# Four transformer blocks on one core: the last heads' queries and keys as one paired matmul, and the last stage's opening beside the last gated batch

## The chip, the cores and the metric

The kernel runs on one core of a Trainium2 chip, in one launch. The metric is the device time in microseconds from the first to the last instruction. TensorE multiplies matrices into PSUM (eight banks of 128 partitions by 512 fp32 values), ScalarE and VectorE read PSUM and SBUF, GpSimd works on SBUF alone, and the Sync engine issues the DMAs. Each engine works through its own instructions in order and waits on semaphores for the others.

## The reference, cut to what matters

The input is x, 4 batches of 512 tokens by 320, with a context of 512 by 192 for each batch. The stages, numbered as in the kernel:

```python
# 0, 1: attention on tokens, then on context: 20 heads of 64; 2: gated feed-forward
# 3, 4: the same with 20 heads of 16;                         5: gated feed-forward
x = attend(layer_norm(x), layer_norm(x), 20 heads of 16) + x      # stage 3
x = attend(layer_norm(x), ctx, 20 heads of 16) + x                # stage 4
# 6: two attentions on 16 + 16 tokens of the context, each weighed by a gate
out = anat_gate * attend(q, k_anat, v_anat) + dis_gate * attend(q, k_dis, v_dis)
x = out @ w_out.T + b_out + x
# 7: attention on the context without a layer norm: 20 heads of 16
q, k, v = heads(x @ Wq), heads(ctx @ Wk), heads(ctx @ Wv)
x = softmax(q k / sqrt(16)) v @ Wo + bo + x
```

## The kernel before, in words

All values are fp32 but for some copies in bf16. x stays in SBUF for the whole kernel. Each engine has its instructions written out by hand: one function for each engine and kind of stage, all looping over the same numbered steps.

A **narrow round** n (stages 3 and 4 are rounds 0 to 7 of run "r3", stage 7 is rounds 0 to 3 of run "r7") treats one batch in 20 steps i. The 20 heads form five groups u of four, one head in each strip of 32 partitions; i = 4u + kb, with kb one of four blocks of 128 keys. In a step TensorE does, in this order (`narrow_steps_pe`): two *row scores* (bf16, queries by 512 keys, for the maxima of a group to be treated six steps later), the *column scores* of this step (`cols_pe`, fp32, 128 keys by 512 queries for four heads, into banks 0 to 3), two more row scores, and then inserts of other work: queries Q, keys K, values V of a chunk, the product of probabilities and values (`mix`), transposes of the output (`turn`, `out`), the output matmul (`y`). ScalarE takes the exponentials of the column scores (`exp_act4`, two halves of 1024 columns) and copies out of PSUM, VectorE the maxima of the row scores (`rows_dve4`), GpSimd casts queries and keys to bf16. The queries of a chunk hold eight heads, and are written twice by ScalarE, each time with a mask that zeroes the other head of each pair of 16 partitions. The last four heads (group 4, columns 256 to 320 of the weights) are laid out twice in the weights, so that chunk 2 is 128 wide as well and one masked activation does (mask column 2). Keys get an additive mask (columns 3 to 5). Queries and keys of chunks 0 and 1 are made in the round before (steps 10 to 18), chunk 2 in steps 0 and 2 of the round itself.

An insert that needs a bank takes the next of four in turn (`Turns.choose`); `wait_free` waits until the bank's former use is over, `wait_full` and `wait_out` for a named item to be written, or taken out again. For the narrow runs the four are banks 4 to 7, and row scores take part in the turn.

The steps of round -1 are the *opening* of a run: transposes of x (steps 3, 4, 6) and of the context (7, 8), Q0 (10), K0 (12), V0 (14), V1 (15), Q1 (16), K1 and the transposed maxima `negm` (18), V2 (19), and from step 14 on the row scores of round 0, four in each step. Run r3 has its opening beside the output phase of stage 2 (`out_pe`, table MEET). Run r7 has it by itself, after the gated stage.

The **gated stage** (6) has steps g = 4n + i for four batches n and token blocks i. In step g TensorE transposes the probabilities of g - 2 (`g_turn_pe`, L1854), makes the scores of g (`g_scores_pe`, L1847, into banks 0 and 1), does a piece of the next batch's set-up, and makes the output of g - 2 (`g_y_pe`, L1901). VectorE takes the probabilities of g - 1 (`g_probs_dve`), the maximum of g and the subtraction (`g_max_dve`), and adds the output of g - 2 (`g_y_dve`, two instructions). The last batch is g = 12 to 15, and 16 and 17 have no scores. The semaphore `sub` counts the subtractions, so its sixteenth means that banks 0 and 1 are read.

The names in the profile: L1059 column scores, L1072 row scores, L1084 maxima, L1251 Q, L1276 K, L1302 V, L1107 the transposed maxima, L1126 mix, L1097 exponentials, L1204 and L1231 transposes of x and of the context, L595 probabilities by values of the wide stages 0 and 1, L351 the feed-forward's output. One fp32 matmul of the program is two passes in the trace, one bf16 matmul or transpose is one.

## Time and profile before

| | us |
|---|---|
| median of 3 runs | 3333.94 (3331.95 to 3334.76) |
| the profiled execution | 3336.34, span 3334.6, mean granted clock 0.989 |
| TensorE busy | 3214.7 (96%) |
| TensorE weight loads, beside the matmuls | 1462.8 (44%) |
| VectorE, ScalarE, GpSimd busy | 1737.4, 1476.5, 805.1 |
| DMA | 62.32 MB, mean 19 GB/s |

Busy time is the union of an engine's instructions. The span is the profiled core's; the time of an execution lies a little above its span. The change touches stages 3, 4, 6 and 7, all after 1763 us.

### The profile page before, as it was taken

What the parts mean: (1) busy time and instruction counts of PE and PEld (TensorE: products, weight loads), DVE (VectorE), ACT (ScalarE), POOL (GpSimd) and SP (SyncE); (2) the same over time, 40 slices, a digit from 0 to 9 for tenths busy, and PEclk for the clock granted to TensorE, in tenths of its full rate; (3) what the DMA queues carried; (4) which work ended last, traced back from release to release, by engine and by line L of the source; (5) the groups of instructions that cost most, each with busy time, mean ns of one, the idle gap of its engine ahead of it and who ended that gap; (6) DMA issues with size and microseconds to landing.
All of it is one profiled execution on the core that took longest, in us unless ns stands there. A gap on an engine that the chain in (4) does not pass through costs nothing.

```text
span 3334.6 us, 39289 instructions
## 1 busy us (share of the span) xinstructions
PE 3214.7 (96%) x15478; PEld 1462.8 (44%) x15478; DVE 1737.4 (52%) x2568; ACT 1476.5 (44%) x1983; POOL 805.1 (24%) x620
## 2 busy tenths in 40 slices
PE   7999999999999999999999999999999999989997
PEld 3344344443434343435444344444434545643443
DVE  2645455454555555552234677777762222656664
ACT  3544444445454545441112656666652112326664
POOL 2544444454554554550000000000000000000000
PEclk9999999999999999999999999999999999989999
DMA  3000000000100000000000000000002000000000
GB/s 110 24 16 20 16 17 20 23 19 20 58 18 18 17 23 13 16 24 20 0 5 26 1 1 1 30 11 6 1 23 65 1 0 33 1 5 6 14 9 17
DMA packets 37284, 62.32 MB, mean 19 GB/s; under 512 B 7024, under 2 KB 24944, under 8 KB 36208
## 3 DMA queue, kind: packets, MB, share of 16 engines
q1 hardware_dynamic: 37104, 59.82, 5.9%
q8 instruction: 125, 2.05, 0.3%
q14 instruction: 55, 0.45, 0.0%
HBM read 57.19 MB, written 2.62 MB: 18 GB/s over the span
## 4 chain that ended last, share of the span: by engine, by line
PE 89%; DVE 5%; ACT 4%; issue 1%; POOL 0%; DMA 0%; ACTq 0%; DVEq 0%; POOLq 0%
PE bank L1589 9%; PE bank L510 9%; PE bank L595 9%; PE bank L1126 7%; PE bank L737 5%; PE bank L351 5%; PE bank L673 5%; PE bank L1059 4%; PE bank L1251 3%; PE bank L676 3%; PE bank L709 3%; PE bank L1276 3%; PE bank L1179 2%; PE bank L533 2%; DVE heads L1084 2%; PE bank L1594 2%
## 5 line engine op out<-in xcount | busy, mean ns | idle before, releaser
L1084 DVE TENSOR_REDUCE heads<-bank 128x1 f32<-128x512 f32 x960 | 598.3, 683 | 237.2 <-PE bank L1072 236.4
L544 DVE TENSOR_REDUCE heads<-bank 128x2 f32<-128x1024 f32 x320 | 392.4, 1226 | 594.7 <-PE bank L533 594.7
L581 POOL TENSOR_TENSOR heads<-heads,probs 128x1024 f32<-128x1024 f32 x160 | 389.5, 2434 | 12.5
L567 ACT ACTIVATE probs<-bank 128x1024 f32<-128x1024 f32 x320 | 328.0, 1025 | 130.3 <-PE bank L519 130.0
L577 POOL TENSOR_TENSOR heads<-probs 128x1024 f32<-128x1024 f32 x80 | 190.7, 2384 | 712.8 <-ACT probs L567 712.8
L510 PE MATMUL bank<-heads 64*128 64x512 f32 x1280 | 335.7, 602 | 0.1
L1059 PE MATMUL bank<-heads 32*128 32x512 f32 x1920 | 296.8, 628 | 25.8 <-ACT weights L1097 10.9
L595 PE MATMUL bank<-probs,values 128*64 128x512 f32 x1280 | 294.0, 601 | 1.4 <-ACT nmT L558 1.0
L1589 PE MATMUL bank<-hT,weights 128*128 128x512 f32 x640 | 291.8, 606 | 1.5 <-issue 1.5
L1097 ACT ACTIVATE weights<-bank 128x1024 f32<-128x1024 f32 x236 | 228.8, 1022 | 96.0 <-PE bank L1059 93.9
L1652 ACT ACTIVATE ctx_in<-bank,b_col 128x512 f32<-128x512 f32 x80 | 55.1, 688 | 419.4 <-PE bank L1594 323.8
L1072 PE MATMUL bank<-heads 32*128 32x512 bf16 x960 | 214.6, 387 | 26.7 <-DVE heads L1084 7.4
L1269 POOL CAST heads<-heads 128x512 bf16<-128x512 f32 x60 | 35.6, 616 | 842.2 <-ACT heads L1260 842.2
L1671 DVE SCALAR_TENSOR_TENSOR mixed<-bank,b_col,ctx_in 128x512 f32<-128x512 f32 x80 | 60.1, 751 | 258.1 <-ACT ctx_in L1652 142.7
L1589 PEld LDWEIGHTS bank<-hT,weights 128*128 128x128 f32 x640 | 119.6, 192 | 165.3 <-issue 163.8
L1097 ACT ACTIVATE probs<-bank 128x1024 f32<-128x1024 f32 x164 | 159.0, 1022 | 62.6 <-PE bank L1059 61.9
L684 ACT COPY heads<-bank 128x512 f32<-128x512 f32 x160 | 93.7, 585 | 187.8 <-PE bank L673 167.7
L351 PE MATMUL bank<-weights,mixed 128*128 128x320 f32 x640 | 175.4, 432 | 0.0
L1072 PEld LDWEIGHTS bank<-heads 32*128 32x128 bf16 x960 | 63.7, 92 | 237.5 <-issue 112.1
L673 PE MATMUL bank<-hT,heads 128*128 128x512 f32 x320 | 161.7, 628 | 0.0
L595 PEld LDWEIGHTS bank<-probs,values 128*64 128x64 f32 x1280 | 85.2, 137 | 172.4 <-issue 168.1
L291 POOL TENSOR_SCALAR vare<-mv 128x4 f32<-128x4 f32 x24 | 4.7, 195 | 577.7 <-DVE mv L277 488.3
(205 smaller groups left out, 4868.9 us busy)
## 6 DMA issues: line engine op xcount, KB each, us to landing
heads<-in_wqk SPq DMA_DIRECT2D x40, 320.0 KB, 2.8
heads<-in_wqk SPq DMA_DIRECT2D x40, 256.0 KB, 2.6
weights<-in_L_xattn_w_ff SPq DMA_DIRECT2D x3, 1600.0 KB, 7.2
weights<-in_L_xattn_ff_w SPq DMA_DIRECT2D x3, 1600.0 KB, 7.1
ctx_in<-in_ctx SPq DMA_DIRECT2D x12, 384.0 KB, 3.7
weights<-in_L_xattn_qkv_q SPq DMA_DIRECT2D x2, 1632.0 KB, 7.4
weights<-in_L_xattn_wo SPq DMA_DIRECT2D x2, 1600.0 KB, 12.2
x_res<-in_x SPq DMA_DIRECT2D x4, 640.0 KB, 13.3
```

The lines of the kernel that those rows point to most:

```text
L351: last = nc.tensor.matmul(M.bank[QUARTER[t]][:, 0:D], v["OT"][c][:, t * P:t * P + P], v["wo"][:, c, :], start=c == 0, stop=c == NF - 1)
L510: nc.tensor.matmul(cols[:, g, :], v["KT"][strip, U % 2, kb * P:kb * P + P], v["QT"][strip, U % 2, :], start=True, stop=False)
L544: nc.vector.tensor_reduce(v["negm"][:, U % 2, qb, :].rearrange("p (g k) -> p g k", g=2)[:, :, 0], M.ROWS[:, :, :], AX.X, ALU.max, negate=T ...
L567: nc.scalar.activation(v["probs"][:, kb, :, :], M.COLS[kb % 2][:, :, :], ACT.Exp, scale=float(r.work[n][0].prm["dh"]) ** -0.5).then_inc(r. ...
L581: nc.gpsimd.tensor_tensor(ps, ps, pr[:, k, :, :], ALU.add).then_inc(r.sem("part"), 1)
L595: last = nc.tensor.matmul(bank[64 * g:64 * g + 64, :], v["V"][:, kb, 2 * u + g, :], v["probs"][:, kb, g, :], start=kb == 0, stop=kb == TB - 1)
L673: last = nc.tensor.matmul(q[:, :], w[:, e, :], M.hT[:, e, :], start=False, stop=e == 1)
L1059: last = nc.tensor.matmul(M.QUAD[:, g, :], v["KT"][strip, u, kb * P:kb * P + P], v["QT"][strip, u, :], start=True, stop=True)
L1072: nc.tensor.matmul(r.bank_of(item, m)[:, :], v["QB"][strip, u, qb * P:qb * P + P], v["KB"][strip, u, :], start=True, stop=True).then_inc(r ...
L1084: nc.vector.tensor_reduce(v["negm"][:, tile, qb, 32 * h + at:32 * h + at + 1], r.bank_of(item, m)[:, :], AX.X, ALU.max, negate=True).then_ ...
L1097: nc.scalar.activation(v["probs"][g % slots][:, 2 * h:2 * h + 2, :], M.QUAD[:, 2 * h:2 * h + 2, :], ACT.Exp, scale=float(r.work[n][0].prm[ ...
L1589: last = nc.tensor.matmul(bank[:, :], v["w1"][:, j, 2 * part + e, :], M.hT[:, e, :], start=first and e == 0, stop=(not first) and e == 1)
```

## The change

Two things are changed. First, `QK_pe4` takes the place of Q2 and K2 in each narrow round: 64 columns of query weights write partitions 0 to 63 of one bank, 64 columns of key weights partitions 64 to 127, by turns. One ScalarE copy takes both into the tile `tail`, and GpSimd writes the masked queries and keys of group 4 from it, 64 partitions at a time, and casts them. V3 moves from step 0 to step 2. Second, the 20 steps of r7's opening are spread over g = 12 to 17 of the gated stage by the tables MEET_FRONT (ahead of the output of g - 2) and MEET_BACK (behind it). While they run, row scores take banks 0 and 1 by turns and the other items banks 6 and 7; the gated outputs keep to banks 2 and 3. The gated stage's second set of W and O moves to other places in SBUF.

```diff
+        self.tail = self.heads[:, 10240:10752]
...
                 if i == 0 and now:
-                    items += [("Q2", n), ("V3", n)]
+                    items += [("QK2", n)]
...
                 if i == 2 and now:
-                    items += [("K2", n)]
+                    items += [("V3", n)]
...
+        class GuestRun(Run):
+            def choose(self, name, n, i):
+                if n >= 0:
+                    return Run.choose(self, name, n, i)
+                if name[0:3] == "row":
+                    return 4 + int(name[7]) % 2
+                return 2 + sum(bank < 4 for bank, _ in self.place.values()) % 2
...
+            if n == 0 and i == 0:
+                for h in (2, 3):
+                    r.wait_out(pe, f"row1_1_{h}", 0)
...
+        def QK_pe4(pe, r, n):
+            s, v, bank = r.work[n][0], n_view(r, n), r.bank_of("QK2", n)
+            r.wait_free(pe, "QK2", n)
+            for e in range(3):
+                for home, name, x, ch in ((bank[0:64, :], "wq", M.hT, CH3), (bank[64:P, :], "wk", kvT(s), keys(s))):
+                    if e < len(ch):
+                        last = nc.tensor.matmul(home, v[name][0:ch[e][1], e, 256:320], x[0:ch[e][1], e, :], start=e == 0, stop=e == len(ch) - 1)
+            last.then_inc(r.full("QK2", n), 1)
+        def QK_act4(act, r, n):
+            r.wait(act, "q_tail", 2 * n)
+            r.wait(act, "k_tail", 2 * n)
+            r.wait_full(act, "QK2", n)
+            nc.scalar.copy(M.tail[:, :], r.bank_of("QK2", n)[:, :]).then_inc(r.free("QK2", n), 1)
+        def Q_tail_pool(pool, r, n):
+            v, low, high = n_view(r, n), slice(0, 64), slice(64, P)
+            r.wait(pool, "cols", 20 * n)
+            r.wait(pool, "q_cast", 5 * n)
+            r.wait_out(pool, "QK2", n)
+            r.wait(pool, "k_cast", 5 * n + 4)
+            for out, which in ((low, 0), (high, 1)):
+                r.wait(pool, "q_tail", 2 * n + which)
+                nc.gpsimd.tensor_scalar(v["QT"][out, 4, :], M.tail[low, :], M.mask[low, which:which + 1], M.mask[low, 6:7], ALU.mult, ALU.add
+                                        ).then_inc(r.sem("q_tail"), 1)
+            r.wait(pool, "q_tail", 2 * n + 2)
+            nc.gpsimd.tensor_copy(v["QB"][:, 4, :], v["QT"][:, 4, :]).then_inc(r.sem("q_cast"), 1)
...
+        MEET_FRONT = {12: (0, 5), 13: (5, 7), 14: (8, 9), 15: (11, 13), 16: (15, 16), 17: (17, 18)}
+        MEET_BACK = {13: (7, 8), 14: (9, 11), 15: (13, 15), 16: (16, 17), 17: (18, 20)}
...
                         g_setup_pe(pe, r, n + 1, SETUP[i][0])
+                    if g == 12:
+                        for k in range(2):
+                            r.wait(pe, f"free{k}", r.count[k])
+                    if g in MEET_FRONT:
+                        narrow_steps_pe(pe, r.guest, -1, *MEET_FRONT[g])
                     if 0 <= g - 2 < 4 * r.N:
                         g_y_pe(pe, r, g - 2)
+                    if g == 15:
+                        r.wait(pe, "sub", 16)
+                    if g in MEET_BACK:
+                        narrow_steps_pe(pe, r.guest, -1, *MEET_BACK[g])
...
                     if 0 <= g - 2 < 4 * r.N:
                         g_y_dve(dve, r, g - 2)
+                    if g == 13:
+                        narrow_begin_dve(dve, r.guest)
+                    if g in MEET_BACK:
+                        narrow_steps_dve(dve, r.guest, -1, *MEET_BACK[g])
...
-                7: Run("r7", stages[7:8], M.NX, 20)}
+                7: GuestRun("r7", stages[7:8], M.bank[4:8] + M.bank[0:2], 20, led=True)}
```

`K_tail_pool` is `Q_tail_pool` for the keys, with the upper half of `tail` and the key mask as the added scalar. The ScalarE loop gets the two tables in the same way as TensorE's, ahead of and behind its exponential.

TensorE, steps 0 to 2 of a round of stage 3 (row scores L1072, column scores L1059, then Q2 and V3 in step 0 and K2 in step 2), before:

```order
L1072 MATMUL bank<-heads 128x512 x2
L1251 MATMUL bank<-hT,weights 128x512 x3
L1302 MATMUL bank<-weights,hT 128x320 x3
L1072 MATMUL bank<-heads 128x512 x2
L1059 MATMUL bank<-heads 128x512 x4
L1072 MATMUL bank<-heads 128x512 x4
L1059 MATMUL bank<-heads 128x512 x4
L1072 MATMUL bank<-heads 128x512 x2
L1276 MATMUL bank<-hT,weights 128x512 x3
L1107 MATMUL bank<-ident,heads 128x128 x4
```

and of the change (row scores are now L1087, column scores L1074, the paired group L1319, values L1359):

```order
L1087 MATMUL bank<-heads 128x512 x2
L1319 MATMUL bank<-hT,weights 64x512 x6
L1087 MATMUL bank<-heads 128x512 x2
L1074 MATMUL bank<-heads 128x512 x4
L1087 MATMUL bank<-heads 128x512 x4
L1074 MATMUL bank<-heads 128x512 x4
L1087 MATMUL bank<-heads 128x512 x2
L1359 MATMUL bank<-weights,hT 128x320 x3
L1122 MATMUL bank<-ident,heads 128x128 x4
```

The values have moved from step 0 to the place of the keys in step 2, and six matmuls with 64 output partitions stand where three queries stood.

TensorE at the end of the gated stage in the change (turns L1912, outputs L1959; of the opening row scores L1087, values L1359, Q L1266, K L1291, transposed maxima L1122), from the output in step 15 to the one in step 17:

```order
L1959 MATMUL bank<-weights,mixed 128x320 x5
L1087 MATMUL bank<-heads 128x512 x4
L1359 MATMUL bank<-weights,cT 128x320 x2
L1912 MATMUL bank<-ident,mixed 128x128 x5
L1087 MATMUL bank<-heads 128x512 x4
L1359 MATMUL bank<-weights,cT 128x320 x2
L1959 MATMUL bank<-weights,mixed 128x320 x5
L1087 MATMUL bank<-heads 128x512 x4
L1266 MATMUL bank<-hT,weights 128x512 x3
L1912 MATMUL bank<-ident,mixed 128x128 x5
L1087 MATMUL bank<-heads 128x512 x4
L1959 MATMUL bank<-weights,mixed 128x320 x5
```

Before, three outputs and two turns follow each other here, and the row scores come only after all of them. VectorE in the same stretch of the change (probabilities L1941 to L1949, output additions L1966 and L1969, maxima L1099), from step 15's addition on:

```order
L1966 TENSOR_TENSOR ysum<-bank,heads 128x320
L1969 TENSOR_TENSOR x_res<-ysum,x_res 128x320
L1099 TENSOR_REDUCE heads<-bank 128x1 x4
L1941 TENSOR_REDUCE mixed<-mixed 128x40
L1943 RECIPROCAL probs<-mixed 128x40
L1946 TENSOR_TENSOR probs<-probs,heads 128x40
L1949 TENSOR_TENSOR mixed<-mixed,probs 128x640
L1099 TENSOR_REDUCE heads<-bank 128x1 x4
L1966 TENSOR_TENSOR ysum<-bank,heads 128x320
L1969 TENSOR_TENSOR x_res<-ysum,x_res 128x320
L1099 TENSOR_REDUCE heads<-bank 128x1 x8
```

The maxima stand behind the additions and behind the last probabilities.

## Rows read from the trace of the kernel before

**Rows 1.** The page: busy time by engine, and the chain by engine.

```profile
PE 3214.7 (96%) x15478; PEld 1462.8 (44%) x15478; DVE 1737.4 (52%) x2568; ACT 1476.5 (44%) x1983; POOL 805.1 (24%) x620
...
PE 89%; DVE 5%; ACT 4%; issue 1%; POOL 0%; DMA 0%; ACTq 0%; DVEq 0%; POOLq 0%
```

**Rows 2.** Timeline, round 1 of stage 3: start, duration, engine, line, passes [idle before].

```profile
1908.12 1.78 PE L1302 MATMUL bank<-weights,hT 108*128 108x320 f32 x6
...
1909.84 1.24 PE L1059 MATMUL bank<-heads 32*128 32x512 f32 x8
...
1915.96 2.85 PE L1276 MATMUL bank<-hT,weights 108*128 108x512 f32 x6
...
1918.64 0.60 PE L1107 MATMUL bank<-ident,heads 128*128 128x128 f32 x4
```

**Rows 3.** Timeline, a round of stage 4, steps 0 to 3.

```profile
2264.65 1.24 PE L1302 MATMUL bank<-weights,cT 96*128 96x320 f32 x4
...
2265.82 1.24 PE L1059 MATMUL bank<-heads 32*128 32x512 f32 x8
...
2272.03 1.94 ACT L1097 ACTIVATE probs<-bank 128x1024 f32<-128x1024 f32 x2 [0.30 <-PE bank L1059]
2272.10 1.98 PE L1276 MATMUL bank<-cT,weights 96*128 96x512 f32 x4
...
2274.46 1.24 PE L1059 MATMUL bank<-heads 32*128 32x512 f32 x8
```

**Rows 4.** Timeline, a wide round: probabilities by values, two heads side by side.

```profile
1215.69 3.65 PE L595 MATMUL bank<-probs,values 128*64 128x512 f32 x16
```

**Rows 5.** Groups of GpSimd, shapes apart: count | busy us, mean ns | idle before.

```profile
L581 POOL TENSOR_TENSOR heads<-heads,probs 128x1024 f32<-128x1024 f32 x160 | 389.5, 2434 | 12.5
...
L1269 POOL CAST heads<-heads 128x512 bf16<-128x512 f32 x60 | 35.6, 616 | 842.2 <-ACT heads L1260 842.2
...
L291 POOL TENSOR_SCALAR vare<-mv 128x4 f32<-128x4 f32 x24 | 4.7, 195 | 577.7 <-DVE mv L277 488.3 <-DVE mv L1511 52.4 <-DVE mv L922 36.9
```

**Rows 6.** Timeline, round 1 of stage 7: column scores of steps 0 and 10.

```profile
3065.93 1.19 PE L1059 MATMUL bank<-heads 32*128 32x512 f32 x8
...
3110.01 1.24 PE L1059 MATMUL bank<-heads 32*128 32x512 f32 x8
```

**Rows 7.** Timeline, gated steps 14 and 15: turn, output, next turn.

```profile
2925.60 0.71 PE L1854 MATMUL bank<-ident,mixed 128*128 128x128 f32 x5
...
2929.39 2.86 PE L1901 MATMUL bank<-values,mixed 128*128 128x320 f32 x10
2932.09 0.71 PE L1854 MATMUL bank<-ident,mixed 128*128 128x128 f32 x5
```

**Rows 8.** Timeline, the opening of stage 7.

```profile
2947.40 1.47 PE L1204 MATMUL bank<-ident,x_res 128*108 128x128 f32 x12
...
2957.50 0.40 PE L1072 MATMUL bank<-heads 32*128 32x512 bf16 x4 [2.26 <-issue]
...
2965.58 4.93 PE L1251 MATMUL bank<-hT,weights 108*128 108x512 f32 x6 [0.20 <-DVE heads L1084]
...
2982.45 2.31 PE L1059 MATMUL bank<-heads 32*128 32x512 f32 x8
```

**Rows 9.** Timeline, VectorE in the same opening.

```profile
2970.86 4.88 DVE L1084 TENSOR_REDUCE heads<-bank 128x1 f32<-128x512 f32 x8 [3.54 <-PE bank L1072]
```

**Rows 10.** Windows: length, busy (instructions) by engine, TensorE's granted clock, DMA.

```profile
2957.00:2961.00 4.00, 2.67 (x11) 1.01 (x11) 2.48 (x4) 0.43 (x1) 0.96 (x2) 0.82 0.00 2
2961.00:2965.00 4.00, 3.85 (x10) 1.48 (x9) 2.65 (x5) 0.43 (x1) 0.00 (x0) 0.50 0.00 0
```

**Rows 11.** Timeline: stage 3's opening, first and last, and an output phase alone.

```profile
1763.91 1.47 PE L1204 MATMUL bank<-ident,xn 128*108 128x128 f32 x12
...
1817.84 2.06 PE L1059 MATMUL bank<-heads 32*128 32x512 f32 x8
...
2780.65 21.70 PE L351 MATMUL bank<-weights,mixed 128*128 128x320 f32 x80
```

More of the change, by code:

```diff
@@ L250, in program @@
              ("VT", 3 * P, "p (c k) -> p c k", dict(c=3)), ("wg", 2, *one), ("sc", 4, *one), ("wgb", 2 * P, "p (c k) -> p c k", dict(c=2)),
[L251 to L254 removed]
+             ("heads8", 8, *one), ("sev", B, *one), ("shift", B, *one),
+             *[(name, 2 * B, "p (b k) -> p b k", dict(b=B)) for name in ("arg", "ge")], ("W", 3 * 640, "p (c k) -> p c k", dict(c=3)))
+        take(M.heads[:, 9216:10752], ("bo", D, *one), ("gate", 2 * B, "p (b k) -> p b k", dict(b=B)))
+        take(M.values[:, 0:1600], ("O", 5 * D, "p (c f) -> p c f", dict(c=5)))
+        take(M.values[:, 3200:5200], ("Kbd", 640, *one), ("Vbd", 640, *one))
         take(M.mixed, ("hT", 2 * 3 * N, "p (s c n) -> p s c n", dict(s=2, c=3)), ("S", 2 * 640, "p (s k) -> p s k", dict(s=2)), ("PT", 640, *one),
@@ L257, in program @@
         take(M.probs[:, 0, 0, :], ("fac", 40, *one), ("gfac", 40, *one))
-        G["W"] = [G["W"][:, k, :, :] for k in range(2)]
-        G["O"] = [G["O"][:, k, :, :] for k in range(2)]
+        G["W"] = [G["W"], M.weights[:, 8512:10432].rearrange("p (c k) -> p c k", c=3)]
+        G["O"] = [G["O"], M.weights[:, 6464:8064].rearrange("p (c f) -> p c f", c=5)]
         GS = M.pair[0].rearrange("p b k -> p (b k)")
@@ L388, in __init__ @@
                         for item in self.step_items(n, i):
-                            bank = self.choose(item[0], i)
+                            bank = self.choose(item[0], n, i)
                             self.place[item] = (bank, count[bank])
@@ L393, in __init__ @@
                         self.upto[steps * n + i] = tuple(count)
-            def choose(self, name, i):
-                return len(self.place) % len(self.banks)
+                self.count = count
+            def choose(self, name, n, i):
+                return len(self.place) % 4
             def sem(self, what):
@@ L1258, in Q_act4 @@
             r.wait_full(act, item, n)
-            for u, which in ((2 * c, 0), (2 * c + 1, 1)) if c < 2 else ((4, 2),):
+            for u, which in ((2 * c, 0), (2 * c + 1, 1)):
                 last = nc.scalar.activation(v["QT"][:, u, :], r.bank_of(item, n)[:, :], ACT.Identity, bias=M.mask[:, 6:7],
@@ L1265, in Q_pool4 @@
             v = n_view(r, n)
-            r.wait_full(pool, f"row{min(2 * c + 1, 4)}_3_3", n - 1)
+            r.wait_full(pool, f"row{2 * c + 1}_3_3", n - 1)
             r.wait_out(pool, f"Q{c}", n)
-            for u in range(2 * c, min(2 * c + 2, 5)):
+            for u in range(2 * c, 2 * c + 2):
                 nc.gpsimd.tensor_copy(v["QB"][:, u, :], v["QT"][:, u, :]).then_inc(r.sem("q_cast"), 1)
@@ L1284, in K_act4 @@
             r.wait_full(act, item, n)
-            for u, which in ((2 * c, 0), (2 * c + 1, 1)) if c < 2 else ((4, 2),):
+            for u, which in ((2 * c, 0), (2 * c + 1, 1)):
                 last = nc.scalar.activation(v["KT"][:, u, :], r.bank_of(item, n)[:, :], ACT.Identity, bias=M.mask[:, 3 + which:4 + which],
@@ L1291, in K_pool4 @@
             v = n_view(r, n)
-            r.wait_full(pool, f"row{min(2 * c + 1, 4)}_3_3", n - 1)
+            r.wait_full(pool, f"row{2 * c + 1}_3_3", n - 1)
             r.wait_out(pool, f"K{c}", n)
-            for u in range(2 * c, min(2 * c + 2, 5)):
+            for u in range(2 * c, 2 * c + 2):
                 nc.gpsimd.tensor_copy(v["KB"][:, u, :], v["KT"][:, u, :]).then_inc(r.sem("k_cast"), 1)
+        def QK_pe4(pe, r, n):
[6 more added lines that the diff above has]
+            last.then_inc(r.full("QK2", n), 1)
@@ new lines, in K_tail_pool @@
+        def K_tail_pool(pool, r, n):
+            v, low, high = n_view(r, n), slice(0, 64), slice(64, P)
+            r.wait(pool, "q_cast", 5 * n + 5)
+            for out, which in ((low, 0), (high, 1)):
+                r.wait(pool, "k_tail", 2 * n + which)
+                nc.gpsimd.tensor_scalar(v["KT"][out, 4, :], M.tail[high, :], M.mask[high, which:which + 1], M.mask[high, 3 + which:4 + which],
+                                        ALU.mult, ALU.add).then_inc(r.sem("k_tail"), 1)
+            r.wait(pool, "k_tail", 2 * n + 2)
+            nc.gpsimd.tensor_copy(v["KB"][:, 4, :], v["KT"][:, 4, :]).then_inc(r.sem("k_cast"), 1)
```

38 lines of the change are left out of this document (21 added, 17 removed).

## The prediction

> **What bounds the kernel now.** I read the page's busy times and its chain first. TensorE is busy 96% of the span and is 89% of the chain [rows 1], so a matmul slot that is saved shows in the time wherever the next step is not held by another engine. Then I read two stretches of the timeline in order of time. The first is the beginning of a narrow round (steps 0 to 2). In a round of stage 3 the values' fourth quarter fills TensorE from 1908.12 to 1909.84 and the third chunk of keys from 1915.96 to 1918.64, with no wait written behind either [rows 2]. In a round of stage 4 the same two take 1.17 us and about 1.8 us [rows 3], fewer passes because the keys come from the context. The second stretch is the seam between the gated stage and the last narrow stage. The gated stage runs a step per 6.49 us, TensorE without a gap: turn and scores 3.79 us, output 2.70 us [rows 7]. Then the opening of stage 7 runs alone, from its first transpose at 2947.40 to the first column score matmul at 2982.45, 35.1 us [rows 8], with TensorE waiting for copies, casts and row maxima in between.
>
> **Part one: one double matmul for two.** In each narrow round three things change on TensorE: the third chunk of queries (six passes) and of keys (six or four) become one group in which a query matmul writes output partitions 0 to 63 and a key matmul 64 to 127, and the fourth quarter of values moves from step 0 to step 2. There are 12 such rounds: 4 whose keys come from the tokens, 8 from the context. Whether the two halves run side by side is the first question. The wide stages have such a form: probabilities by values, 128 rows by 64 columns, two heads by turns into the two halves of a bank. 16 passes last 3.65 us [rows 4], 0.23 us each, while a full-width pass of 512 columns costs 2.68/6 = 0.45 us [rows 2]. So the pair overlaps 1.9 times, and the group costs what the queries alone did.
>
> The Trainium skill (TensorE: Matmul & The Clock Gate, "Why this matters for your kernels") gives three column tiles of 32 a speedup of 2.38 rather than 3. Scaled to two tiles that is an estimate of 1.6, and by it the groups would cost some 6 us more over the 12 rounds; the trace's 1.9 decides, and the sum goes by it.
>
> In a round of stage 3 the whole key chunk is gained, 2.68 us: step 0 loses 1.72 us of values, step 2 changes 2.68 us for 1.72 us. In a context round step 0 loses 1.17 us. In step 2 the 1.8 us become 1.17 us, but there the next step's score matmuls must follow the exponentials: these run from 2272.03 for 1.94 us, and TensorE follows some 0.15 us later, at 2274.12, where it now follows at 2274.46 [rows 3]. So only 0.3 us of the 0.65 us is gained, 1.48 us for the round. Sum: 4 x 2.68 + 8 x 1.48 = 22.6 us. If nothing held step 2 it would be 25.4 us.
>
> What is added lies elsewhere. ScalarE does one copy in place of two activations. GpSimd does four masked copies of 64 x 512 with two casts. No row has that operation. Its bounds are the smallest tensor_scalar, 0.195 us, and the addition of 1024 columns with two inputs, 2.43 us; the nearest is the 512-column cast, 0.62 us, since it too reads one tensor of 512 columns, and I take 1.0 us for the second operation and the scalars [rows 5]. The tail then takes 4 x 1.0 + 2 x 0.62 = 5.2 us (2.0 to 11 us by the bounds). Its first user is the row scores of the fifth group in step 10. From step 0 at 3065.93 to step 10 at 3110.01 are 44.1 us [rows 6]; the copy out of the bank is there about 6.5 us after step 0 begins, so 37 us are free and the tail costs nothing. Without that cover each microsecond of it would cost 12. Behind it on GpSimd are only the casts of the next round, whose inputs come after step 10. The QK bank is freed by a 0.6 us copy right behind the exponentials, before the fourth row matmul of step 1 needs it. Values in step 2 wait for the same row maximum that the keys waited for.
>
> **Part two: the opening beside the last gated batch.** Four gated steps of 6.49 us and two half steps without scores (3.25 us each) are 32.5 us. The opening's TensorE work at full clock is 20 transpose passes 2.2 (12 in 1.47 busy [rows 8]), queries 2 x 2.68, keys 2 x 1.8, values 3 x 1.17, row scores 6 x 0.4, the maxima's transposes 0.5: 17.6 us. Were TensorE all that counts, the six steps would last 50.1 us from 2912.6 (2932.09 less 3 x 6.49), and end 19.8 us before 2982.45. They will not. The row scores of the opening get two banks (in place of a turn through four), and VectorE reduces one bank in 0.61 us [rows 9]. The third row matmul needs the first reduction's end, the fourth the second's, so TensorE leaves a group of four some 1.9 us after VectorE begins it. VectorE begins late: the order has the output's two additions (2 x 0.49) ahead of three groups, the probabilities (2.4) ahead of one. Step by step the six groups hold TensorE 2.9, 3.3, 2.9, 2.2, 2.9 and 2.6 us, 16.8 in place of 2.4. That makes 50.1 + 14.4 = 64.5 us, the first column score matmul at 2977.1: 5.4 us gained at full clock. The two memsets of values and the one of maxima fall into step 13, where VectorE has the slack of a longer step. They cost nothing; without that slack they would cost up to 4 us. The transfers are unchanged, and the stage's weights land during earlier gated batches.
>
> Now the clock. In the old opening TensorE was busy 2.67 of 4 us, and the granted clock fell to 0.50 [rows 10], the 1.2 GHz level. The second chunk of queries took 4.93 us [rows 8] for work of 2.68; over the opening's queries, keys and values the loss is about 7 us up to 2982.45, and 4 us after it, in the first steps of round 0. In the new one TensorE idles 14 us of the last 32: busy 55%, less than before the old fall. So I expect the clock to fall again and to cost about the same 7 us there and 4 us after. The seam then gives -5.4 + 7 = +1.6 us. The nearest row from the other side is stage 3, whose opening already lies beside an output phase: from the first transpose at 1763.91 to 1817.84 are 53.9 us, of which the output's 80 passes are 21.7 [rows 11], so the opening adds 32.2 us. Added to the gated stage's 34.8 us that gives 67.0 against 69.9 us, -2.9. But stage 3 has four banks. I take +1.6, with -9.4 (no fall at all: -5.4 less the old 4 us after the start) and +6.5 (the half clock through the whole second half) as the ends.
>
> The same page of the Trainium skill puts mid-kernel drops down to long idle gaps between bursts. The longest gap in the old opening was 2.26 us [rows 8] and short pieces followed, yet the clock fell. By the page's rule the new opening, with gaps of at most 2.1 us, would keep the full clock: that is the second rival below.
>
> **Sum.** The profiled execution took 3336.34 us (span 3334.6), 2.4 us over the median 3333.94. 3336.34 - 22.6 + 1.6 = 3315.3 there, 3333.94 - 21.0 = 3312.9 as a median.
>
> **Rivals.**
> 1. The forecast: both parts as above, 3312.9, own range 3307 to 3319. Chance 0.60.
> 2. The merged opening keeps the full clock: -22.6 - 9.4 = 3301.9. For it: the gated matmuls are dense and sit between the gaps. Against it: the fall at 67% busy. Chance 0.17.
> 3. The shortened steps are not short: VectorE's maxima or the exponentials hold step 0 too, and half of part one is lost, -11 + 1.6 = 3324.5. For it: in the context round the exponentials already bind in step 2. Against it: in step 0 they end a microsecond ahead of TensorE. Chance 0.13.
> 4. The halves do not overlap. The group then costs 12 or 10 passes, 5.4 or 4.5 us for 2.7: nothing is gained in 4 rounds and 0.3 us lost in 8, +2 + 1.6 = 3337.5. Against it: rows 4. Chance 0.06.
> 5. Slower: the GpSimd tail becomes late for step 10, and row scores wait. It is reached when one masked copy takes 9 us (4 x 9 + 1.2 = 37), and the kernel is slower than before from 9.5 us on; at 10 us it would lose 12 x 4.2 = 50, 3363. Against it: four times the largest row. Chance 0.02. Another 0.02 is for what I don't see.
>
> **How the numbers follow.** The time is that of rival 1. The range takes rivals 1 and 2 whole and most of 3's way: 3301 to 3322. A measurement of this kernel tells 0.2% (6.7 us) from no change. Rivals 1 to 3 are faster by more (0.90, and 0.01 of the unseen), rival 4 lies within (0.06), the rest is slower (0.03).
>
> **What would show it.** The 64-column matmuls start in pairs, a self round's group lasting about 2.7 us. Steps 0 to 2 of a stage 3 round shorten by 2.7 us and of a stage 4 round by 1.5 us. GpSimd's masked copies are near 1 us and nobody waits for them. Between the tenth and the last gated output, row matmuls wait for VectorE about 2 us each group, and the granted clock falls in the second half of the seam; the first column score matmul comes some 71 us (64.5 + 7) after the turn in step 12. Wrong would be: pairs that start one after the other, TensorE waiting for a GpSimd cast, or a seam at full clock.

## The result, and the profile after

| | before | after |
|---|---|---|
| median of four executions, us | 3334.35 (3331.95 to 3337.23) | 3310.36 (3306.34 to 3313.49) |
| the profiled execution, us | 3336.34, span 3334.6 | 3307.46, span 3305.7 |

The ratio is 0.9929 with a 95% interval of 0.9917 to 0.9942: 23.7 us faster (19 to 28), where 21 were forecast. The four executions after came as 3307.46, 3306.34, 3313.26 and 3313.49 us, with mean granted clocks of 0.991, 0.991, 0.989 and 0.989; the profiled one is of the quicker pair. The spans of the two profiled executions differ by 28.9 us, and 4.65 of those lie ahead of stage 3, in code that the change does not touch.

The page after, its lines on busy time and on the chain (of before: [rows 1]):

```profile
PE 3186.8 (96%) x15478; PEld 1449.8 (44%) x15478; DVE 1739.6 (53%) x2568; ACT 1461.1 (44%) x1971; POOL 844.4 (26%) x668
...
PE 89%; DVE 5%; ACT 4%; issue 1%; POOL 0%; DMA 0%; ACTq 0%; DVEq 0%; POOLq 0%
```

TensorE has the same number of instructions and is busy 27.9 us less, nearly the whole difference of the spans: the work has become shorter, while its idle time is about as before (118.9 us for 119.9). GpSimd is busy 39 us more and has no share of the chain.

The timeline of TensorE after, at the points that cut the span into stretches: the first transpose of stage 3's opening, its first column scores, the first transpose of the gated stage, the turn of step 12, the first column scores of stage 7:

```profile
1759.26 0.93 PE L1219 MATMUL bank<-ident,xn 128*108 128x128 f32 x7
...
1813.27 1.84 PE L1074 MATMUL bank<-heads 32*128 32x512 f32 x8
...
2780.78 0.38 PE L1768 MATMUL bank<-ident,heads 128*96 128x128 f32 x2
...
2891.14 0.77 PE L1912 MATMUL bank<-ident,mixed 128*128 128x128 f32 x5
...
2962.24 2.21 PE L1074 MATMUL bank<-heads 32*128 32x512 f32 x8
```

The same points before stand at 1763.91 and 1817.84 [rows 11], 2802.18 and 2912.56 (in the same views) and 2982.45 [rows 8]. So:

| stretch | before | after | difference | forecast |
|---|---|---|---|---|
| start to stage 3's opening | 1763.91 | 1759.26 | -4.65 | 0 |
| that opening | 53.93 | 54.01 | +0.1 | 0 |
| rounds of stages 3 and 4, feed-forward | 984.34 | 967.51 | -16.8 | -16.6 |
| gated stage to the turn of step 12 | 110.38 | 110.36 | 0 | 0 |
| seam | 69.89 | 71.10 | +1.2 | +1.6 |
| stage 7, round 0, step 0 to Q0 of step 10 | 44.84 | 40.67 | -4.2 | -1.5 |
| the rest of stage 7, each of 3 rounds | | | -1.5 | -1.5 |

(The forecast column: 4 x 2.68 + 4 x 1.48 = 16.6 for stages 3 and 4.) Now a round of stage 3, steps 0 to 2, in the timeline of TensorE after (before: [rows 2]):

```profile
1898.40 1.24 PE L1074 MATMUL bank<-heads 32*128 32x512 f32 x8
...
1899.67 2.80 PE L1319 MATMUL bank<-hT,weights 108*64 108x512 f32 x12
...
1902.40 1.24 PE L1074 MATMUL bank<-heads 32*128 32x512 f32 x8
...
1907.26 1.24 PE L1074 MATMUL bank<-heads 32*128 32x512 f32 x8
...
1908.53 1.89 PE L1359 MATMUL bank<-weights,hT 108*128 108x320 f32 x6
```

Twelve passes take 2.73 us (1899.67 to 1902.40), where the full-width queries took six passes and as long. Steps 0 to 2 last 4.00, 4.86 and 3.53 us; before they lasted 5.68, 4.85 and 4.49. The round is 87.94 us for 90.6, as forecast (2.68). In a round of stage 4 the halves stand in rows of their own, since their inputs have different names, and start together (before: [rows 3]):

```profile
2246.77 0.64 PE L1319 MATMUL bank<-hT,weights 108*64 108x512 f32 x1 [0.36 <-DVE heads L1099]
2246.77 0.64 PE L1319 MATMUL bank<-cT,weights 96*64 96x512 f32 x1
...
2248.54 1.02 PE L1319 MATMUL bank<-hT,weights 106*64 106x512 f32 x2
2249.49 0.39 PE L1087 MATMUL bank<-heads 32*128 32x512 bf16 x2
```

Its steps 0 and 2 are 4.42 and 3.34 us (5.56 and 3.78 before), the round 85.41 for 86.92. GpSimd's tail in the round of stage 3 above:

```profile
1903.43 1.62 POOL L1338 TENSOR_SCALAR heads<-heads,mask 64x512 f32<-64x512 f32 x2 [6.98 <-ACT heads L1327]
1905.12 0.61 POOL L1341 CAST heads<-heads 128x512 bf16<-128x512 f32 x1
1905.83 1.65 POOL L1349 TENSOR_SCALAR heads<-heads,mask 64x512 f32<-64x512 f32 x2
1907.54 0.61 POOL L1352 CAST heads<-heads 128x512 bf16<-128x512 f32 x1
```

A masked copy is 0.8 us, the tail 4.7 (1903.43 to 1908.15). No wait of TensorE in the narrow rounds names GpSimd; the one that does, 2.9 us, is in a wide stage.

The seam, a part of TensorE's timeline from the tenth gated output on:

```profile
2923.72 0.39 PE L1087 MATMUL bank<-heads 32*128 32x512 bf16 x2
2925.50 0.38 PE L1087 MATMUL bank<-heads 32*128 32x512 bf16 x1 [1.40 <-DVE heads L1099]
...
2926.41 1.70 PE L1359 MATMUL bank<-weights,cT 96*128 96x320 f32 x4
...
2931.63 2.50 PE L1359 MATMUL bank<-weights,cT 96*128 96x320 f32 x4
2933.92 4.63 PE L1959 MATMUL bank<-weights,mixed 128*128 128x320 f32 x10
...
2941.39 5.49 PE L1266 MATMUL bank<-hT,weights 108*128 108x512 f32 x6
```

And windows of the same stretch (busy time by engine, then the granted clock):

```profile
2926.00:2934.00 8.00, 7.12 (x19) 3.76 (x20) 5.97 (x11) 1.18 (x3) 0.00 (x0) 0.58 0.00 1
2934.00:2938.00 4.00, 4.00 (x10) 2.61 (x9) 0.00 (x0) 0.42 (x1) 0.00 (x0) 0.56 0.00 0
2938.00:2947.00 9.00, 7.39 (x15) 2.73 (x14) 3.47 (x6) 0.08 (x1) 0.00 (x0) 0.66 0.00 0
2947.00:2961.00 14.00, 10.12 (x38) 4.99 (x37) 8.89 (x15) 3.45 (x6) 2.34 (x4) 0.97 0.00 1
2961.00:2969.00 8.00, 8.00 (x25) 2.27 (x23) 2.63 (x5) 2.36 (x3) 0.00 (x0) 0.57 0.00 0
```

Each group of four row matmuls waits for VectorE: the first from 2923.72 to 2926.41. The six hold TensorE 2.69, 2.52, 2.90, 2.09, 2.69 and 2.36 us, 15.3 in all (16.8 forecast). The clock falls to 1.2 GHz twice between 2926 and 2947 (0.58 and 0.56 in the first two windows, then 0.66): the gated output takes 4.63 us for 2.86, the queries 5.49 for 2.74. Six inserts (V0 and V1, two turns, the output, Q1) are 7.1 us longer in their rows than at full clock; the row matmuls between them add about another. It falls again at 2961, under the first column scores.

How long the seam lasts depends on where the clock falls: seven traces have this same opening, and their seams are 71.10 us (three of them), 68.63 (no_turns) and 72.04 to 72.06 (v3_stays, seam_alone, tail16). So a difference of less than 3.5 us between the seams of two unlike kernels shows little by itself.

### The profile page after: what moved, and what is told of

Its sections match the earlier page's. It is cut to its first block, busy times and chain, and to the rows that moved or that the text cites. A ratio compares the mean times of both kernels' runs of the same rounds, so it can differ in the third digit from the quotient of the medians.

```text
span 3305.7 us, 39329 instructions
## 1 busy us (share of the span) xinstructions
PE 3186.8 (96%) x15478; PEld 1449.8 (44%) x15478; DVE 1739.6 (53%) x2568; ACT 1461.1 (44%) x1971; POOL 844.4 (26%) x668
## 4 chain that ended last, share of the span: by engine, by line
PE 89%; DVE 5%; ACT 4%; issue 1%; POOL 0%; DMA 0%; ACTq 0%; DVEq 0%; POOLq 0%
PE bank L513 9%; PE bank L1644 9%; PE bank L598 9%; PE bank L1141 7%; PE bank L740 5%; PE bank L353 5%; PE bank L676 5%; PE bank L1074 5%; PE bank L679 3%; PE bank L712 3%; PE bank L1194 2%; PE bank L536 2%; DVE heads L1099 2%; PE bank L1649 2%; PE bank L1087 2%; PE bank L669 2%
## 5 line engine op out<-in xcount | busy, mean ns | idle before, releaser
L1099 DVE TENSOR_REDUCE heads<-bank 128x1 f32<-128x512 f32 x960 | 599.0, 683 | 218.8 <-PE bank L1087 218.2
L1074 PE MATMUL bank<-heads 32*128 32x512 f32 x1920 | 295.0, 628 | 25.8 <-ACT weights L1112 10.4
L1087 PE MATMUL bank<-heads 32*128 32x512 bf16 x960 | 217.0, 384 | 31.0 <-DVE heads L1099 14.4
L1284 POOL CAST heads<-heads 128x512 bf16<-128x512 f32 x48 | 28.7, 625 | 786.6 <-ACT heads L1275 786.6
L1644 PEld LDWEIGHTS bank<-hT,weights 128*128 128x128 f32 x640 | 118.9, 191 | 163.3 <-issue 161.9
L1087 PEld LDWEIGHTS bank<-heads 32*128 32x128 bf16 x960 | 64.4, 92 | 246.4 <-issue 112.3
```

Of the source, the lines that this page charges most:

```text
L1074: last = nc.tensor.matmul(M.QUAD[:, g, :], v["KT"][strip, u, kb * P:kb * P + P], v["QT"][strip, u, :], start=True, stop=True)
L1087: nc.tensor.matmul(r.bank_of(item, m)[:, :], v["QB"][strip, u, qb * P:qb * P + P], v["KB"][strip, u, :], start=True, stop=True).then_inc(r ...
L1099: nc.vector.tensor_reduce(v["negm"][:, tile, qb, 32 * h + at:32 * h + at + 1], r.bank_of(item, m)[:, :], AX.X, ALU.max, negate=True).then_ ...
L1644: last = nc.tensor.matmul(bank[:, :], v["w1"][:, j, 2 * part + e, :], M.hT[:, e, :], start=first and e == 0, stop=(not first) and e == 1)
```

## The experiments

The kernels were run in three sets of four, each set on one chip beside the kernel before, and each ratio is to that. The medians before were 3331.91 us (first set), 3331.95 (second) and 3332.4 (third). The changed kernel itself was run again in the third set only.

| run | median, us | ratio to before, 95% |
|---|---|---|
| pair_alone | 3312.9 | 0.9944 (0.9931 to 0.9956) |
| seam_alone | 3334.91 | 1.0009 (1.0 to 1.0018) |
| no_turns | 3312.11 | 0.9941 (0.9928 to 0.9955) |
| v3_stays | 3327.97 | 0.9986 (0.9976 to 0.9995) |
| split_rows | 3306.73 | 0.9919 (0.9905 to 0.9932) |
| three_split | 3301.33 | 0.9905 (0.9892 to 0.9919) |
| fill | 3307.62 | 0.9925 (0.9912 to 0.9939) |
| tail16 | 3585.35 | 1.0756 (1.0741 to 1.0771) |
| apart | 3342.56 | 1.003 (1.0018 to 1.0041) |
| split_fill | 3305.5 | 0.9924 (0.991 to 0.9937) |
| after_again | 3312.58 | 0.9943 (0.993 to 0.9955) |
| three_split_again | 3302.61 | 0.9912 (0.9898 to 0.9925) |

### Each part by itself

pair_alone keeps the serial opening of stage 7 and has part one. 

> Only the paired queries and keys with the GpSimd tail; the opening of stage 7 stands alone as before. Theory (the gain is TensorE slots in steps 0 and 2 of 12 rounds): 22 to 23 us under before, about 3311; rounds of stage 3 shorter by 2.65 us, context rounds by 1.5 us; the seam from the turn of step 12 to the first column scores 69.9 us as before. Rival (the seam gives a good part of the gain): less than 15 us under before.

seam_alone has the merged opening, with Q2, K2 and V3 as before. 

> Only the opening beside the last gated batch; queries, keys and values of the rounds as before. Theory: the seam lasts 71 us instead of 69.9 and the ten steps after it are some 2.7 us shorter by the clock, so 0 to 3 us under before, no difference that can be told. Rival (the merge is worth TensorE's idle time of the old opening): 8 us or more under before.

Measured: 0.9944 and 1.0009. In pair_alone's trace the rounds are those of the changed kernel (87.94 and 85.41 us), the seam is 69.89 us as before, and the first ten steps of stage 7 are 3.9 us shorter than before, not 1.5. In seam_alone's the seam is 72.05 us and those ten steps are 1.15 us shorter. So part one is the whole gain, and part two brings none that can be measured. seam_alone was expected 0 to 3 us below before and came out 3.0 us above it (0 to 6), a small miss; its seam is 2.2 us longer by the trace, which is within the spread of the seams. The ratio of pair_alone is a little less than its rounds give (18.7 us for 22.8), but its interval reaches to 23, and its profiled execution lost 3.3 us to a stretch of half clock in the gated set-up (113.66 us for 110.36). Seven of the fourteen traces have that stretch and seven do not; of three_split, the first trace has it and the second does not.

### Does the gain come from the halves overlapping?

no_turns issues all queries of the group first, then all keys:

```diff
-            for e in range(3):
-                for home, name, x, ch in ((bank[0:64, :], "wq", M.hT, CH3), (bank[64:P, :], "wk", kvT(s), keys(s))):
+            for home, name, x, ch in ((bank[0:64, :], "wq", M.hT, CH3), (bank[64:P, :], "wk", kvT(s), keys(s))):
+                for e in range(3):
```

> The changed kernel with the matmuls of the paired group in another order: three of the queries, then those of the keys, instead of by turns. Theory (only neighbours in the order that write different column halves overlap): the group lasts 12 or 10 passes, 5.1 or 4.3 us instead of 2.7, and the kernel is 4 x 2.5 + 8 x 1.7 = 24 us slower than the changed one, about 3334. Rival (TensorE overlaps the halves in whatever order they come): as the changed kernel, 3310.

That theory fell: the time is within 2 us of the changed kernel's (3310.36, and 3312.58 when run again). In the timeline of a self round:

```profile
1897.31 3.71 PE L1319 MATMUL bank<-hT,weights 108*64 108x512 f32 x12
1900.94 0.39 PE L1087 MATMUL bank<-heads 32*128 32x512 bf16 x2
```

The group lasts 3.63 us: 0.9 more than by turns, but 1.8 less than two halves of 2.72 us in a row. In a context round it lasts 2.78 us for 2.72, and its passes are listed so:

```profile
2247.15 1.51 PE L1319 MATMUL bank<-hT,weights 108*64 108x512 f32 x3 [0.36 <-DVE heads L1099]
2248.07 0.65 PE L1319 MATMUL bank<-cT,weights 96*64 96x512 f32 x1
2248.49 0.59 PE L1319 MATMUL bank<-hT,weights 106*64 106x512 f32 x1
2248.55 0.59 PE L1319 MATMUL bank<-cT,weights 96*64 96x512 f32 x1
```

The first row merges three passes; the third of them starts at 2248.06, beside the first key pass. So two query passes stand alone, then keys start beside queries, ahead of some that the program issued before them. The order in the group need not be by turns for most of the gain. It did not show whether the gain is from overlap at all; apart does. It leaves the queries of the group in step 0 (half 0) and puts the keys (half 1) behind the next step's first row scores:

```diff
                 rows_pe4(pe, r, n, i, (0, 1))
+                if i == 1 and now:
+                    QK_pe4(pe, r, n, 1)
                 if now:
                     cols_pe(pe, r, n, i, (2, 3, 0, 1)).then_inc(r.sem("cols"), 1)
                 rows_pe4(pe, r, n, i, (2, 3))
                 if i == 0 and now:
-                    QK_pe4(pe, r, n)
+                    QK_pe4(pe, r, n, 0)
```

> The changed kernel with the query matmuls of the paired group left in step 0 and its key matmuls moved behind the next step's first two row scores, so that other work stands between the two halves. With the halves in one group but all queries first (an earlier run) the group lasted 3.63 us, by turns 2.73. Theory (the two halves are cheap only because their passes run beside each other, and they do so only when both are queued together): each half now costs its full passes, 6 x 0.45 and 6 or 4 x 0.45 us, the 4 self rounds lose about 2.7 us and the 8 context rounds 1.8 us, 25 us in all, 3335 us or 1.00 of before. Rival (the gain of part one comes from half-width matmuls or from the values' move, not from running beside each other): 3308 to 3313 us, ratio 0.993.

Its timeline in a self round:

```profile
1904.58 2.79 PE L1320 MATMUL bank<-hT,weights 108*64 108x512 f32 x6
1907.30 0.39 PE L1087 MATMUL bank<-heads 32*128 32x512 bf16 x2
1907.62 2.79 PE L1320 MATMUL bank<-hT,weights 108*64 108x512 f32 x6
```

Six half-width passes by themselves take 2.72 us, as long as twelve that overlap. Rounds are 90.97 and 87.59 us: 4 x 3.03 + 8 x 2.18 = 29.6 us, and the medians differ by 30.0 from the changed kernel in the same set. The theory had 25: it left out the two row matmuls between the halves, which now take 0.32 us by themselves (1907.30 to 1907.62), where in the changed kernel they start together with the column scores (1902.40). Half-width matmuls and the move of V3, without the overlap, gain nothing here: the kernel is slower than before.

### Where the values stand

v3_stays leaves V3 in step 0, behind the paired group. 

> The changed kernel with the values' fourth quarter left in step 0. Theory (a step lasts at least 3.3 us, column scores 1.3 then exponentials 1.94 and the way back): step 0 is as long as before, step 2 falls to 3.3 us from 4.5 or 3.8 us, so part one is worth 4 x 1.2 + 8 x 0.44 = 8 us instead of 22.8, and the kernel takes about 3325. Rival (the saved slots count wherever they are): as the changed kernel, 3310.

Measured 0.9986: 4.7 us faster than before (1.7 to 8), at 3327.97 us, nearer to the theory's 3325 than to the rival's 3310. Steps 0 to 2 of a self round are 5.82, 4.86 and 3.34 us, of a context round 5.70, 4.85 and 3.35: step 2 ends at the same 3.34 us in both, held by the exponentials, with no insert left to shorten. Rounds are 89.48 and 86.69, so the pair alone brings 4 x 1.1 + 8 x 0.23 = 6.2 us, and the move of V3 into step 2 the other 4 x 1.54 + 8 x 1.28 = 16.4. The two belong together: pairing frees step 2, and V3 has to fill it.

### How much cover GpSimd has

tail16 does each masked copy 16 times:

```diff
-                nc.gpsimd.tensor_scalar(v["QT"][out, 4, :], M.tail[low, :], M.mask[low, which:which + 1], M.mask[low, 6:7], ALU.mult, ALU.add
-                                        ).then_inc(r.sem("q_tail"), 1)
+                for again in range(16):
+                    ins = nc.gpsimd.tensor_scalar(v["QT"][out, 4, :], M.tail[low, :], M.mask[low, which:which + 1], M.mask[low, 6:7], ALU.mult, ALU.add)
...
```

(the part left out lets each copy wait for the one before it), and the same for the keys. 

> The changed kernel with each of the four masked copies on GpSimd done 16 times, one after the other. It tests the cover of the GpSimd tail. Measured: one is 0.8 us, the tail 4.7 us, and from the copy out of the bank to the row scores of step 10 some 33 to 37 us are free. Theory: the tail becomes 4 x 16 x 0.8 + 1.2 = 52 us, 15 to 19 us more than the cover, each of the 12 rounds gets longer by that much, and row scores of step 10 wait for GpSimd: +180 to +230 us, 3490 to 3540 us. Rival (other users of the QK copies come earlier or GpSimd is also late for the next round's casts, or the masked copy is faster when repeated): anywhere else; at no loss at all the cover would be larger than 52 us.

In its timeline, GpSimd and then TensorE at step 10:

```profile
1929.53 27.47 POOL L1339 TENSOR_SCALAR heads<-heads,mask 64x512 f32<-64x512 f32 x32 [6.98 <-ACT heads L1327]
...
1958.06 28.18 POOL L1355 TENSOR_SCALAR heads<-heads,mask 64x512 f32<-64x512 f32 x32
1986.31 0.61 POOL L1363 CAST heads<-heads 128x512 bf16<-128x512 f32 x1
```

```profile
1987.02 0.61 PE L1087 MATMUL bank<-heads 32*128 32x512 bf16 x2 [19.79 <-issue]
1987.03 2.31 PE L1074 MATMUL bank<-heads 32*128 32x512 f32 x8
```

The tail is 57.4 us (a copy 0.86, not 0.8) and TensorE idles 19.8, so 57.4 - 19.8 = 37.6 us were free: the 37 of the prediction. The time is 273 us over the changed kernel's 3312.58 (measured in the third set, on another chip), 23 per round, where 180 to 230 were expected. The expected tail was 52 us, and it is 57.4. The twelve waits are 20.0 us in the mean (239.9 in all), and the rest goes with the clock: after the wait TensorE runs at half clock (column scores 2.31 us for 1.24), and the round shown is 22.2 us longer for a wait of 19.8. The cover is as the prediction had it; what lies beyond it costs more than its own length.

### The seam: VectorE and the clock

Three kernels change only the merged opening. split_rows puts the third and fourth row matmuls of a step behind that step's insert:

```diff
-                rows_pe4(pe, r, n, i, (2, 3))
+                late = n == -1 and isinstance(r, GuestRun)
+                if not late:
+                    rows_pe4(pe, r, n, i, (2, 3))
...
+                if late and i != 17:
+                    rows_pe4(pe, r, n, i, (2, 3))
```

(step 17's follow the gated output.) 

> The changed kernel, but in the last narrow stage's opening the third and fourth row matmuls of each step are issued behind that step's queries, keys, values or output matmuls, not ahead of them. It tests what the opening's waits for VectorE cost and what the clock costs. In the changed kernel's seam (turn of step 12 to the first column score matmul) 71.1 us were measured: 64.5 by the sum at full clock, some 7 for the clock. Theory: the waits are real and TensorE's work covers them when it stands between; about 1.2 us are gained in each of 6 groups, the seam falls by 6 to 9 us to some 63 us, and as the gaps shorten the clock falls later or not at all, so 3300 to 3305 us. Rival A, TensorE's waits are only moved (VectorE is the bound of the seam, as its maxima, additions and probabilities queue there): the seam stays within 2 us of 71, 3310 us. Rival B, the clock falls as before whatever the gaps are: seam 66 to 68, 3306 us.

three_split also gives the row scores banks 0, 1 and 3, and the last gated outputs bank 2 alone. 

> As split_rows, and the opening's row scores turn through three banks in place of two (the last gated batch's outputs use one bank for it). Theory (a bank that VectorE has not yet reduced is what the third row matmul waits for): with three banks the third waits for nothing and the fourth for one reduction; with the work in between the waits nearly vanish, the seam is 1 to 3 us shorter than with split_rows alone unless one bank for the outputs makes the next output wait for VectorE's additions (0.5 us each); 3299 to 3304 us. Rival (VectorE's queue is the bound): as split_rows, or 1 to 2 us worse from the single output bank.

fill adds two matmuls between a step's row matmuls, whose result nothing reads:

```diff
+                if n == -1 and isinstance(r, GuestRun) and i >= 14:
+                    v0 = n_view(r, 0)
+                    for _ in range(2):
+                        nc.tensor.matmul(M.bank[3][:, :], v0["wq"][0:108, 0, 0:128], M.hT[0:108, 0, :], start=True, stop=True)
```

> The changed kernel, with two matmuls of 512 columns added to each of the opening's steps 14 and later, between the second and third row matmul, where TensorE waits for VectorE; their result goes to a bank that nothing reads (the last gated batch's outputs use one bank instead of two). It adds work and computes nothing with it. It tests whether the clock falls because of TensorE's idle time. At full clock the two last 1.8 us, about as long as the wait that they fill. Theory (what TensorE does before decides the clock): the fall at about 35 us into the seam and the one behind it vanish or are shorter by half, the seam is 64 to 67 us in place of 71.1 though work was added, 3304 to 3308 us. Rival (the fall does not depend on these gaps, or the added work does not fit in them): seam 72 to 80 us, 3312 to 3320 us.

Seams: changed kernel 71.10 us, split_rows 62.91, three_split 60.90, fill 65.35. In fill's timeline the added matmuls are L1395, 1.98 us where the changed kernel's third row matmuls wait for 0.78 to 1.40 us:

```profile
2926.78 0.39 PE L1087 MATMUL bank<-heads 32*128 32x512 bf16 x2
2927.10 1.98 PE L1395 MATMUL bank<-hT,weights 108*128 108x512 f32 x4
2929.12 0.38 PE L1087 MATMUL bank<-heads 32*128 32x512 bf16 x1
```

Its windows over the seam's second half and what follows:

```profile
2924.00:2944.00 20.00, 19.75 (x67) 9.54 (x66) 12.47 (x21) 3.70 (x8) 1.17 (x2) 1.00 0.00 0
2944.00:2963.00 19.00, 17.53 (x78) 7.03 (x78) 12.77 (x21) 6.33 (x8) 4.07 (x6) 1.00 0.00 1
2963.00:2969.00 6.00, 6.00 (x30) 2.96 (x20) 3.26 (x6) 2.36 (x3) 1.40 (x3) 0.53 0.00 0
```

Twelve matmuls, some 11.5 us of useless work, were added, and the seam became 5.75 us shorter, with the clock at 1.00 to its end. Its 65.35 us are near the 64.5 us that the prediction gave the seam at full clock. They are also 3.3 us below the shortest seam of any trace with the same opening unfilled, and none of those seven kept the clock. So the falls inside the seam do follow from TensorE's idle time in it. One came at 2963 all the same, behind a wait of 1.1 us for the exponentials. The rival (they come whatever fills the gaps, 72 to 80 us) is out. In the medians the gain cannot be told: fill is 24.3 us below before, the changed kernel 23.7 and, run again, 19.8, with intervals that overlap.

split_rows hides the waits and loses less to the clock: its seam fell to the theory's 63 us, though its time, 3306.73 us, is a little above the 3300 to 3305 expected. The three banks remove more (3301.33 us, as expected). This is three_split_again's timeline, where a wait of 1.48 us is still followed by a slow output:

```profile
2933.36 0.38 PE L1087 MATMUL bank<-heads 32*128 32x512 bf16 x1 [1.48 <-DVE heads L1099]
2933.68 4.65 PE L1963 MATMUL bank<-weights,mixed 128*128 128x320 f32 x10
```

The third set has a kernel with both remedies at once, and the best one beside the changed kernel on one chip. split_fill is split_rows with one such matmul in each of four steps. 

> The kernel with the split row scores (seam 62.9 us, two falls of the clock in and right behind it), with one matmul added per opening step from 15 on, ahead of the late row scores; its result goes to a bank that nothing reads (the last gated outputs use one bank). Four are added, 0.9 to 1.0 us each at full clock, where TensorE waits 0.2 to 1.2 us. Theory (the clock falls because of TensorE's waits, as the run with two such matmuls per step kept 1.00 through the seam): no fall in the seam, which gains 2.5 us, less 1 to 2 us of added work that no wait hides: seam 60.5 to 63 us, the opening steps behind it 1 us shorter, 3302 to 3306 us. Rival (the falls come anyway): seam 64 to 67 us, 3308 to 3311 us.

after_again: 

> The changed kernel unchanged, beside the next run on the same chip. Its first times came in two pairs, 3306.3 and 3307.5, 3313.3 and 3313.5 us. Expected 3307 to 3312 us; the ratio to before 0.992 to 0.994.

three_split_again: 

> The kernel with the split row scores and three banks for them once more, beside the changed kernel on one chip. Theory (its seam is 10.2 us shorter than the changed kernel's by the trace, 60.9 for 71.1, though its set-up ahead of it was caught 3 us longer): 3298 to 3303 us, 6 to 10 us below the changed kernel. Rival (the first measurement owed it to a favourable placing of the clock's falls): within 3 us of the changed kernel.

split_fill's windows:

```profile
2927.00:2955.00 28.00, 24.81 (x86) 11.64 (x86) 18.63 (x33) 5.25 (x10) 2.89 (x5) 1.00 0.00 1
2955.00:2965.00 10.00, 8.54 (x26) 2.28 (x25) 4.20 (x7) 2.36 (x3) 0.00 (x0) 0.50 0.00 0
```

The first fall was gone, the one at the end stayed. Its seam is 64.31 us, 1.4 longer than without the added work, its median within 1.3 us of split_rows in the set before. Its time is as the theory had it and its seam as the rival had it, and nothing was won that can be told. The changed kernel came out at 3312.58 us, 0.6 us above the 3307 to 3312 expected. three_split_again took 3302.61 us (3301.63 to 3303.3) beside 3312.58 (3309.3 to 3316.29) of the changed kernel: 10.0 us less, what the seams say (60.90 for 71.10), with ranges that do not meet. That is the version to keep; against before it is 0.9912, and 0.9905 when it was first run.

## Why the prediction was right, step by step

**The halves overlap 1.9 times.** Right: 2.73 us for twelve passes, and apart shows that without overlap all of part one's gain is lost and more. The place from which it was read, the wide stages' 64-column matmuls [rows 4], was the right one. The 1.6 estimated from the Trainium skill (TensorE: Matmul & The Clock Gate, "Why this matters for your kernels") was too low here: six passes alone take 2.72 us, twelve 2.73, which is 2.0.

**2.68 us per self round, 1.48 per context round.** Right to 0.05 us. The limit in step 2 of a context round, where the exponentials hold the next scores, was read from [rows 3], and the step ends at 3.34 us with V3 in it or without (3.35 in v3_stays, where column scores wait for the exponentials). Rival 3 (half of it lost) is refuted by the round lengths.

**The tail on GpSimd.** The masked copy is 0.8 us for 1.0, the tail 4.7 for 5.2, the cover 37.6 for 37.

**The seam at full clock, 64.5 us.** Borne out within 1.5 us: by fill, which took 65.35 us at 1.00, and by the sum, since the measured groups (15.3 us for 16.8) make it 63.0, and some 8 us for the clock make 71. No run has the changed kernel's seam itself at full clock.

**The clock in the seam, about 7 us.** Right in place, cause and nearly in size: 7.1 us in six inserts. The old and the new seam have about the same mean granted clock (0.86 and 0.87), as the prediction had it. Rival 2, the full clock, is out. This is also where the Trainium skill was weighed (TensorE: Matmul & The Clock Gate, "Why this matters for your kernels"), which puts mid-kernel drops down to long idle gaps: by it the clock would have stayed up, and this trace does not agree, since the clock fell with no gap over 1.4 us in the rows above.

**The clock after the seam.** This is the term that was mis-sized. The prediction put 4 us of loss there, before and after alike; it was some 5.4 us before and 2.9 us after, so the first ten steps of stage 7 became 4.2 us shorter and not 1.5. The ten steps as a window, first before (granted clock 0.87, with a part of it at 0.50), then after (0.92), each with the row of step 2's insert:

```profile
2982.45:3026.01 43.56, 39.56 (x231) 15.66 (x232) 26.72 (x44) 24.76 (x30) 1.23 (x2) 0.87 0.03 10
2993.70:3000.50 6.80, 6.80 (x24) 2.94 (x20) 2.45 (x5) 2.72 (x3) 0.62 (x1) 0.50 0.00 0
2994.78 3.78 PE L1276 MATMUL bank<-cT,weights 96*128 96x512 f32 x4
```

```profile
2962.24:3001.63 39.39, 35.59 (x230) 13.41 (x230) 26.64 (x44) 23.23 (x28) 4.30 (x6) 0.92 0.04 11
2973.70 1.34 PE L1359 MATMUL bank<-weights,cT 96*128 96x320 f32 x4
```

Before, the clock was at half at the start of step 0 and once more from 2993.7 to 3000.5, over step 2 and the start of step 3. Steps 0, 2 and 3 took 7.27, 6.35 and 3.95 us; at full clock they would take about 5.2 (a context round's 5.56 less its wait), 3.63 and 3.37 (as in seam_alone). After, only step 0 met the half clock (6.91 us, for 4.00 in fill, whose clock was up there). In pair_alone step 0 took 4.00 us, but steps 2 and 3 took 5.68 and 3.97. In seam_alone step 0 took 9.41, and the rest ran at full clock. So how much shorter the ten steps are in each (3.9 and 1.15 us) depends on where its trace met the half clock. Why the falls lie where they do in each kernel isn't settled.

**What the sum owes to chance.** The medians differ by 23.7 us here and 19.8 in the third set (3332.4 and 3312.58). The forecast of 21 lies between, and that it comes within 3 us of either is in part luck: the clock after the seam alone was off by 2.7 us, and the changed kernel's executions spread over 10 us (3306.34 to 3316.29). Their mean granted clock goes with the time (0.991 in the two quicker of the first four, 0.989 in the two slower). Its two traces have the same set-up (110.36 us) and the same seam, so they do not show where the slower executions lose it.

## What to carry to other kernels

Two matmuls that each use half of the output partitions cost one here when issued by turns (2.73 us for 2.72), somewhat more when all of one half come first (3.63), and two with two row matmuls between the halves (5.44). Most of the gain came only because the slot that pairing empties was filled again (16.4 of 22.6 us), so look for the step that another engine holds before you count it. When an opening is laid beside other work, the waits come along: splitting each group of row matmuls around that work, and giving the groups one bank more, was worth 10 us here. A wait on TensorE can cost more than its own length, by the half clock behind it: 22.2 us for a wait of 19.8 in tail16.

## What was unexpected of the hardware

- Passes of matmuls that write different halves of the partitions overlap though they are not neighbours in the program: all queries before all keys cost 3.63 us for twelve passes, and 2.78 for ten, where serial passes of 0.45 us would be 5.4 and 4.5. The first key pass started beside the third of six query passes, though the program issues it behind all six. What decides how far apart in the program two passes may stand was not measured, and stays open; with two row matmuls between the halves there was no overlap.
- Added matmuls made a stretch shorter: with 11.5 us of them in the seam it was 5.75 us shorter, as they filled waits of 6.8 us and the clock stayed at 2.4 GHz.
- After an idle stretch of 19.8 us the first column scores took 2.31 us for 1.24.
